# Turning attention weights and rows by SP's transposing loads, with powers of two on ACT and a second output bank

## The reference, cut to what matters

```python
h = top_k_tokens(x, w)                       # 125 -> 88 rows of 192 in each of 32 sequences
h = h + attn(layernorm(h))                   # 12 heads of 16, everything quantized
h = h + experts(layernorm(h))                # 16 experts, the best 4 of each row, weighted

def log_int_softmax(x, scale):               # in attn, on the scores; all values are whole numbers
    x_int = x / scale - max(x / scale);  x0_int = floor(-0.6931 / scale)
    q = floor(x_int / x0_int);           r = x_int - x0_int * q
    z = r * (r + b_int) + c_int
    exp_int = floor(z * exp2(30 - q))
    ratio = round(sum(exp_int) / exp_int)
    big = floor(log2(ratio)), one more where ratio >= 1.5 * 2**big
    return exp2(-big), or 0 where big >= 16
```

## Time and profile before

| | |
|---|---|
| median of 3 runs | 767.3 us (765.73 to 770.07) |
| profiled execution, its own time | 765.98 us |
| its span | 764.2 us |
| busy: PE, DVE, ACT, POOL | 441.1, 560.7, 490.9, 447.3 us |
| chain that ended last, by engine | PE 22%, ACT 18%, SPq 17%, DVE 17%, issue 12% |
| moved by DMA | 93.65 MB |

### The profile page before, as it was taken

How to read it: one execution, slowest core, us unless ns; L and a number is a source line. 1 busy time by engine, 2 the same in 40 slices (tenths; PEclk the granted TensorE clock), 3 DMA queues, 4 the chain that set the end, 5 groups by cost and what they waited for, 6 DMA issues and landing times.

```text
span 764.2 us, 14352 instructions
## 1 busy us (share of the span) xinstructions
PE 441.1 (58%) x3943; PEld 294.3 (39%) x3943; DVE 560.7 (73%) x1426; ACT 490.9 (64%) x874; POOL 447.3 (59%) x554
## 2 busy tenths in 40 slices
PE   0695353746456463745633335567687787788454
PEld 0242132333334242433422224345465565466343
DVE  3686897899999999898998645545676665666746
ACT  0055876798897969788774535255666655666664
POOL 9781725247587987979777653555455444445500
PEclk9997555555555555555555567679999988979669
DMA  9469999999011030210101164425444344431078
GB/s 186 55 145 293 318 318 294 321 293 285 13 55 53 22 93 30 79 40 6 51 11 40 52 102 86 101 72 126 97 92 93 83 95 86 91 81 34 1 291 317
DMA packets 149613, 93.65 MB, mean 123 GB/s; under 512 B 77122, under 2 KB 143643, under 8 KB 149538
## 3 DMA queue, kind: packets, MB, share of 16 engines
q1 hardware_dynamic: 139266, 75.04, 38.7%
q0 software_dynamic: 10272, 17.70, 7.3%
HBM read 23.61 MB, written 61.24 MB: 111 GB/s over the span
## 4 chain that ended last, share of the span: by engine, by line
PE 22%; ACT 18%; SPq 17%; DVE 17%; issue 12%; another core or an unknown queue 6%; POOL 4%; DMA 2%; DVEq 0%; ACTq 0%; POOLq 0%
SPq L483 7%; PE pX L1920 6%; PE pS L1904 6%; PE pP L1904 4%; SPq L475 3%; POOL w1s L597 2%; DVE S_e L1462 2%; ACT stage L1059 2%; DVE negmx L1381 2%; SPq L537 2%; DMA w2s<-expert_rows 2%; SPq L432 2%; PE pP L1796 1%; ACT stage L1044 1%
## 5 line engine op out<-in xcount | busy, mean ns | idle before, releaser
L782 POOL DMA_INDIRECT expert_rows<-stage,dest x118 | 118.6, 1005 | 130.3 <-ACT stage L1044 74.4
L1593 DVE TENSOR_SCALAR arena<-pS 128x512 f32<-128x512 f32 x59 | 40.6, 689 | 80.7 <-remote 59.9
L1920 PE MATMUL pX<-w2s,stage 128*128 x472 | 65.1, 270 | 39.8 <-ACT stage L1044 32.1
L706 POOL DMA_INDIRECT region<-rows,slots x60 | 68.0, 1134 | 16.5 <-issue 15.9
L597 POOL TENSOR_TENSOR w1s<-stage,w1s 128x384 f16<-128x384 f32 (+8 forms) x72 | 67.3, 935 | 11.4 <-ACT w1s L866 6.4
L1920 PEld LDWEIGHTS pX<-w2s,stage 128*128 128x128 f16 x472 | 43.6, 106 | 57.3 <-issue 53.6
L1052 ACT ACTIVATE arena<-pS 64x256 f32<-64x256 f32 x59 | 22.1, 375 | 59.5 <-PE pP L1904 30.1
L1796 PE MATMUL pP<-idb,S_p 128*88 128x128 bf16 x192 | 25.8, 316 | 46.3 <-DVE S_p L1414 46.3
L1674 PE MATMUL pX<-arena,WA 128*128 128x384 f16 x86 | 34.4, 501 | 30.5 <-ACT arena L878 21.2
L1823 PE MATMUL pP<-WpT,oq 128*128 128x192 bf16 x72 | 15.4, 349 | 60.7 <-ACT pTs L996 57.7
L706 POOL DMA_INDIRECT region<-arena,slots x36 | 41.0, 1138 | 15.6 <-issue 8.5
(11 more groups left out here) (442 smaller groups left out, 1620.7 us busy)
## 6 DMA issues: line engine op xcount, KB each, us to landing
region<-zrow SPq DMA_DIRECT2D x45, 800.0 KB
w1s<-expert_rows SPq DMA_DIRECT2D x16, 384.0 KB, 7.7
stage<-in_L_ffn_w_dram SPq DMA_DIRECT2D x24, 192.0 KB
stage<-in_L_ffn_w_dram SPq DMA_DIRECT2D x8, 384.0 KB
w2s<-expert_rows SPq DMA_DIRECT2D x8, 384.0 KB, 11.8
arena<-in_x_dram SPq DMA_DIRECT2D x4, 672.0 KB
expert_rows<-stage,dest POOLq DMA_INDIRECT x118
out_dram<-xsel SPq DMA_DIRECT2D x8, 198.0 KB
```

What stands on the lines that cost most here:

```text
L706: pool.indirect_dma_start(region_rows, bass.IndirectOffsetOnAxis(ap=slots[q % 3][:, i, m:m + 1], axis=0), rows[q % 3][:, i, :].bitcast(I16 ...
L782: pool.indirect_dma_start(y_dram, bass.IndirectOffsetOnAxis(ap=dest[(st - 7) % 8][:, j:j + 1], axis=0), ysb[b][:, j, :], None, bounds_chec ...
L1593: dve.tensor_scalar(lin[r], hidLC[r], -6.0 * XS * WS, 8.0 * XS * WS, ALU.max, ALU.min).then_inc(s["l_done"], 1)
L1920: ins = pe.matmul(y_ps[:, j, :], lhs, w2s[:, kind, bass.ds(k_, 1), :].rearrange("p o f -> p (o f)"), start=n == 0, stop=n == 4)
```

## The change

It has seven parts.

1. The twelve transposes of S_p on PE and ACT's two copies go. SP issues in each slot one transposing load pTs<-S_p of 128x1536 values (`turn_p`). S_p gets a row pitch of 128, its pad zeroed once by POOL.
2. `transpose_x` and `evac_xT` go for quads 1 to 7, `turn_rows` and `evac_rT` for quads 0 to 6; SP issues three transposing loads of 128x384 values for each (`turn_x_by_load`, `turn_by_load`). xT keeps the tiles whole, so the tail of v is projected in three small pieces.
3. The fills come as 11 shares, each the same 256 rows of all 16 experts (3.28 MB), two before the slots and then one in each slot with i = 0 or i = 2, up to slot 12. POOL's sends wait for the shares that they need.
4. ACT makes S_pow, straight behind S_g, instead of DVE.
5. ACT copies o8 to oq, straight behind o8, instead of POOL.
6. The low halves of the routed rows of quads 0 to 5 are made by DVE (`low_tail`), ahead of S_ratio in slots with (st - 7) % 3 = 0. `scale_bias` moves from slots with i = 0 to i = 1, `norm_x` and `high_x` from i = 2 to i = 1, and POOL's work on an expert pair is cut in two (8 parts with i = 0, 4 with i = 1).
7. y_ps alternates between pX and pO from step 7 on, so PE waits for the copy before the last one.

The diff, cut to its core:

```diff
@@ block.sync
+            def turn_x_by_load(q):
+                sp.wait_ge(s["low1"], 2 * q + 2)
+                sp.wait_ge(s["xr_filled"], fill(3 * q - 4, "v", 1) + 1 if q >= 2 else 11)
+                for i in range(3):
+                    sp.dma_start(xT[:, :, 128 * i:128 * i + 128], xw[:, i, :], transpose=True).then_inc(s["x_turned"], 16)
...
+            def turn_p(st):
+                sp.wait_ge(s["p_ready"], st)
+                sp.wait_ge(s["o_ready"], st - 1)
+                sp.dma_start(pTs[:, :, :], S_p[:, :, :].rearrange("p h n -> p (h n)").bitcast(BF16),
+                             transpose=True).then_inc(s["p_turned"], 16)
...
+            for st in range(NT + 1):
+                q, i = st // 3, st % 3
+                if i == 1 and 0 <= q - 2 < LASTQ:
+                    turn_by_load(q - 2)
+                if st >= 1:
+                    turn_p(st)
+                if i == 2 and q + 2 < NQ:
+                    turn_x_by_load(q + 2)
+                if i != 1 and 2 + 2 * q + i // 2 < REGION // STEP:
+                    fill_share(2 + 2 * q + i // 2)
+                if i == 1 and q + 2 < E // 2:
+                    sp.wait_ge(s["stage_low"], 12 * (q + 1))
+                    load_pair(q % 2, 2 * q + 4)
@@ block.scalar, slot
-                    act.wait_ge(s["pow_ready"], n)
+                    act.wait_ge(s["rho_ready"], n)
                     act.activation(S_g[:, :, :], S_w[:, :, :], ACT.Identity, scale=k(K_IX),
                                    bias=k(K_GB)).then_inc(s["g_ready"], 1)
+                    act.wait_ge(s["g_ready"], n + 1)
+                    if st >= 1:
+                        act.wait_ge(s["e_ready"], n)
+                    act.activation(S_pow[:, :, :], S_g[:, :, :], ACT.Identity, scale=128.0,
+                                   bias=k(K_PB)).then_inc(s["pow_ready"], 1)
...
                     act.activation(o8[:, :], pO[:, 0:384], ACT.Identity, scale=k(K_CO)).then_inc(s["o8_ready"], 1)
+                    act.wait_ge(s["o8_ready"], n - 1)
+                    if st >= 3:
+                        act.wait_ge(s["proj_ready"], n - 2)
+                    act.activation(oq[:, :], o8[:, :], ACT.Copy).then_inc(s["oq_ready"], 1)
...
-                if i == 0 and st <= 18:
+                if i == 1 and st <= 19:
 ...
...
-                if 1 <= st <= NT:
...
@@ block.tensor, products
                     if st >= 6:
-                        pe.wait_ge(s["y_out"], p - 5)
+                        pe.wait_ge(s["y_out"], p - 5 if st - 5 <= Y_APART else p - 6)
```

More of the change, by code:

```diff
@@ L318, in audio_tower @@
         s = {n: sem(n) for n in names}
+        share_filled = [sem(f"share_filled{i}") for i in range(2)]
         row_sent = [sem(f"row_sent{i}") for i in range(3)]
@@ new lines, in turn_by_load @@
+            def turn_by_load(q):
+                sp.wait_ge(s["low2"], 2 * q + 2)
+                if q >= 1:
+                    sp.wait_ge(s["xr_filled"], fill("gate", q - 1) + 1)
+                    sp.wait_ge(s["ter_copied"], q)
+                for i in range(3):
+                    sp.dma_start(xTr[:, :, 128 * i:128 * i + 128], rows[q % 3][:, i, 0:2 * C],
+                                 transpose=True).then_inc(s["turned"], 16)
+            def turn_p(st):
[3 more added lines that the diff above has]
+                             transpose=True).then_inc(s["p_turned"], 16)
@@ L501, in sent @@
+            turn_by_load(LASTQ - 1)
             def sent(quads):
@@ L589, in low_pair @@
                 parts += [(slice(96, 128), 3, w2s, 1536, C, 0)]
-                for done, (rows, kind, ws, at, width, to) in enumerate(parts):
+                for done, (rows, kind, ws, at, width, to) in list(enumerate(parts))[span]:
                     if done or not first:
@@ L737, in send, with low_part @@
                     for q_, n_ in pending[:count]:
+                        if n_ == 0:
+                            pool.wait_ge(s["rows_zeroed"], 16 * 5)
+                            for parity in range(2):
+                                pool.wait_ge(share_filled[parity], 16 * len(range(parity, shares_of(q_), 2)))
                         send_row(q_, n_)
                     del pending[:count]
[L741 to L744, removed]
                 if st <= NT:
                     send((3, 0, 3)[i] if st < NT else 2)
[L747 to L752, removed]
+                def low_part(span):
+                    upto = 3 * q + 1
+                    low_pair(q, q * 2, st // 3 % 2, st == 0,
+                             [sum(q_ % 3 == ring for t in range(upto) for q_, _ in sends(t)) for ring in range(3)], span)
                 if i == 0 and st < NT:
[L755 to L756 removed]
+                    low_part(slice(0, 8))
+                if i == 1 and st < NT:
+                    low_part(slice(8, 12))
                 if st // 3 + 1 < NQ:
@@ L1394, in slot @@
                     dve.tensor_tensor(pr8[:, :], proj_ps, pA[:, :], ALU.mult).then_inc(s["pr_a"], 1)
-                if nxt and i == 0:
-                    evac_xT(0, fill(st, "x", 0))
                 if nxt and i == 2:
                     quant_v(q + 1, 0, fill(st, "v", 0))
+                if quad_at(st, TURN) is not None and quad_at(st, TURN) < TAILQ:
+                    low_tail(quad_at(st, TURN))
                 if 1 <= st <= NT:
@@ L1423, in slot @@
                                              ALU.subtract).then_inc(s["rho_ready"], 1)
-                    dve.wait_ge(s["e_ready"], n)
-                    dve.tensor_scalar(S_pow[:, :, :], S_g[:, :, :], 127.0 - MOST, 128.0, ALU.add, ALU.mult).then_inc(s["pow_ready"], 1)
-                if nxt and i == 0:
-                    evac_xT(2, fill(st, "x", 2))
                 if nxt and i == 2:
@@ L1435, in slot @@
                                              ALU.add).then_inc(s["resid"], 1)
-                if quad_at(st, TURN) is not None:
-                    evac_rT(quad_at(st, TURN), 0)
-                if i == 2 and st // 3 + 2 < NQ:
+                if i == 1 and st // 3 + 2 < NQ:
                     norm_x(q + 2)
@@ L1809, in slot @@
                     rank_rows(quad_at(st, RANK))
-                if quad_at(st, TURN) is not None:
-                    for m in range(2):
-                        turn_rows(quad_at(st, TURN), m)
                 if nxt and i == 1:
```

187 lines of the change are left out of this document (87 added, 100 removed).

## The result

The changed kernel takes 770.6 us (median, 766.54 to 774.63), the kernel before 767.2 beside it: ratio 1.0046, interval 1.0027 to 1.0065. That is slower by about half of a per cent, inside the bound of no change, where 761 was forecast. The profiled execution's span went from 764.2 to 768.0 us, so +3.8, and this is what the two traces have to explain; the forecast for the same sum was -6.4.

What follows compares the result with a forecast made beforehand. The prediction took ACT's and DVE's nearly level chains to bound the slots. Slots +6.6, between slots and steps -3, steps -10 gave -6.4 on 765.98: 759.6, with 1.3 more as a median 761 us; range 745 to 780.

Steps and rivals of the forecast that it cites:

- What bounds the slots: In each slot, ACT's chain to S_sq and DVE's chain to S_e nearly level; DVE's net -4.4 us a quad costed at nothing.
- The rival that DVE was the bound: S_e does not wait for ACT's squares, so each quad takes DVE's 4.4 us less: 723 us; chance 0.10.
- The price of a quad: Steady quad: +1.8 us, from -0.65, +1.9 and +0.6 with i = 0, 1, 2; ACT's additions 1.89 us a slot.
- Slots 3, 4 and 5: Early slots: -4.1 from earlier expert weights, +4.06 where ACT is last already, +0.7 us.
- SP's loads: Transposing load of S_p: 2.46 us to issue, 4.7 from issue to use; some 7 us of room.
- the +1 of the sum: Fills against loads of S_p in SP's queue: +1 us, bounds 0 and 2.
- The rival of late loads: S_p's DMA stands behind a share, each load late by about 3 us in 8 slots: +24, 785 us; chance 0.15.
- The estimate of 1.1 us from the Trainium skill: Load of S_p priced from transposes as fast as other DMAs, 350 to 400 GB/s; the +1 would be 0.
- Between slots and steps: DVE's 3.94 us wait for the gates shrinks, as rows are turned sooner and POOL sends earlier: -3 us.
- The steps: From step 7 on, a second bank takes 0.49 us off each of some 20 PE waits for ACT's copy: -10 us.
- The rival that the bank gives nothing: PE's issue holds the steps, and the wait for ACT becomes a wait for issue: +3.6, 771 us; chance 0.20.
- a sign of being wrong: In the steps, issue waits grown by what the waits for ACT lost.

Runs made afterwards that it cites:

- d_pow_dve: The changed kernel with S_pow made by DVE again; ratio 0.9807 to the kernel before, on the 675 us chip.
- e_pow_dve_pool_oq: The changed kernel with S_pow back on DVE and oq back on POOL; ratio 0.9748, 740.6 us beside 760.7 for the kernel before.
- c2_hold_sends: The changed kernel with one wait added in POOL's slot 23, until DVE has ranked quad 5's gates; ratio 0.9992 to before, on a 761 us chip.
- h_pool_stands: The changed kernel with one POOL wait more per slot, until ACT's oq is there; ratio 0.9926 to the kernel before.
- g_pairs: The changed kernel with POOL waiting before every second send of quad 4, so at most two are under way; ratio 1.0097 to before.

## Why the prediction was wrong, point by point

**What bounds the slots: right.** ACT's square and DVE's own chain were level, and the operations given to ACT turned S_e into a wait for ACT. The rival that DVE was the bound (723 us) is out. d_pow_dve and e_pow_dve_pool_oq show it from the other side: with ACT's additions gone, the saving on DVE appears at once.

**The price of a quad: right in kind, too high by 1 us.** With i = 1 the forecast was g + 11.0; the trace has 10.99. The two additions came to 1.21 (S_pow) and 0.57 us (oq), 1.78 for 1.89. What was missing is mostly on DVE's side: from S_e to the next S_g it was 5.4 and 6.8 us with i = 0 and 1 instead of the 5.6 and 7.3 of the forecast, and with i = 0 and 2 ACT was 0.2 us sooner each. So +0.8 for +1.8. Slots 3, 4 and 5 moved by -4.3, +4.0 and +0.6 us, as forecast (-4.1, +4.06, +0.7); slot 22 gave 1.9 us of its 3.7. At slot 22 the trace stands at +5.45, where the sum for all slots was +6.6.

**SP's loads: right, the latency too high by 1 us.** From issue to use 3.7 us for the 4.7 taken (its own terms, 2.46 and 2.33, give 4.8); the issue of a load with twice the values took 1.42 us, not 2.46. One collision with a fill cost 1.1 us in slot 13 (17.51 for 16.40), the +1 of the sum. The rival of late loads did not come true, but its mechanism is there as soon as slots get shorter (d_pow_dve). The estimate of 1.1 us from the Trainium skill (Advanced Engine Details and Errata, X-Bar Transpose) was nearer to the 1.42 of the trace than the 2.46 scaled by size; not so where fills were under way. No row here times the transfer of such a load alone.

**Between slots and steps: this step failed.** The prediction put it as "POOL, without the waits for oq, sends earlier ... I take -3". The direction was wrong: the stretch from slot 22 to the first step load is 10.4 us longer. POOL does not even send earlier: its last send of quad 4 ends at 421.64, at 421.54 before. What changed is that the nine sends stand in one train, and the gates, whose product PE ends after the third of them, reach DVE 9.2 us later. That POOL's timing is the cause is shown from two sides: a wait in POOL alone takes S_e of slot 23 back to 12.5 us behind that of slot 22 (c2_hold_sends; 21.3 in the changed kernel), and another brings the first step load 10.1 us forward (h_pool_stands). How the length of a train enters is not shown: in the kernel before, with the product ending under the third of six sends, the gates were there within 1.6 us. The gates' wait is not all of it either: c2_hold_sends ends it, and DVE stands 11.49 us before the counts instead. The range for this term went from 0 to -5; the text never asked what POOL would run beside once nothing held it back, though the earlier trace rows already had a wait of 3.94 us with a remote releaser in just that place.

**The steps: right in size, not by the working.** -10 was forecast; the trace has -12.1, the run without the bank 9 us. The rival that the bank gives nothing is out where before takes 761. But the working took 0.49 us off each of some 20 waits for ACT, a third of the 32.1 us; 23.6 us of them went, and about 20 us of waits for issue took their place, which the prediction had named as a sign of being wrong. That 10 came out near 9 is in part luck, and where before takes 675 the same bank gave about nothing.

Together: -1.1 from the slots, -2.1 from the steps, and +13.4 from the stretch between, on a forecast of -6.4: +3.8.

## What to carry to other kernels

When an engine loses its waits, look at what it will do in one go, and beside whose work: a wait that seems to cost nothing may be what keeps DMA issues in short groups. Before giving work to the engine that is not busiest, measure both chains that end at the same point, from one common mark; 36 busy us against 41 in a quad said nothing about who came last. And a change of seven parts can hold a gain of 2.5% and lose it again in two of them, so each part wants a run of its own.

## What the runs showed of the hardware

Where the kernel before takes 761 to 767 us, results of PE that end while POOL issues a train of indirect DMAs (one each 1.28 us) can reach DVE and ACT late. The four longest waits of DVE between slots and steps ended 1.6 to 2.4 us after the train's last send: 8.94 us behind nine sends, 8.87 behind twelve, 11.49 in c2_hold_sends and 16.43 in g_pairs. The end of the train is not the rule for all, though. ACT read its o8 in the middle of three of these trains, 3.2 us after PE's product in the changed kernel, 3.1 in c2_hold_sends and 9.9 in g_pairs. In h_pool_stands DVE read the gates 1.7 us after PE's product and the next ones 2.9 us after it, each time with the train still going, and in the kernel before no wait stood at the gates in a train of six.

PE's records show the products done, and in the train of twelve other work of DVE and ACT ran on (442.17, 440.02). With one send in flight (g_pairs) and with two issued just before (c2_hold_sends), the gates were read within 0.3 us of PE's product. Where before takes 675 us the traces of four kernels, three of them also traced on the other kind of chip, have no wait over 2 us with a remote releaser on DVE or ACT. What in the chip makes the difference, what it is that is held, and how many sends it takes, was not tried and stays open.
